# Two steps' horizontal distances and caps in one instruction each, and loads in batches of eight steps, in the main loop of a deformable convolution

## What is computed

```python
py = off_y + hs[None, None, :, None] + ky[None, :, None, None]   # one offset for each tap and pixel
px = off_x + ws[None, None, None, :] + kx[None, :, None, None]
...
return v00 * w00 + v01 * w01 + v10 * w10 + v11 * w11             # bilinear, zero outside the image
...
sampled = sampled * mask[:, None]
out = jnp.einsum('bckhw,ock->bohw', sampled, w.reshape(O, C, KK))
```

## Time and profile before

| | |
|---|---|
| median of 3 runs | 2331.67 us (2330.77 to 2337.22) |
| profiled execution | span 2334.2 us; its own time is not listed apart from the span |
| busy | PE 1539.5 (66%), DVE 1558.4 (67%), ACT 1449.8 (62%), POOL 606.7 (26%) |
| main loop | from about 680 to 2105 us of the span |
| TensorE clock granted, mean | 0.846 |

### The profile page before, as it was taken

One profiled execution on the slowest core, in us unless ns is written; L12 is line 12 of the kernel. 1 busy time (PEld: TensorE's weight loads), 2 busy tenths in 40 slices (PEclk: granted clock), 3 DMA queues, 4 the chain that ended last, 5 costly groups with the idle time before them and its releaser, 6 DMA issues. The chain is left out here.

```text
span 2334.2 us, 61913 instructions
## 1 busy us (share of the span) xinstructions
PE 1539.5 (66%) x24206; PEld 1050.0 (45%) x24207; DVE 1558.4 (67%) x1718; ACT 1449.8 (62%) x2219; POOL 606.7 (26%) x1168
## 2 busy tenths in 40 slices
PE   4755980000008888888898898898888898891620
PEld 4632330000006666666665566666665666660310
DVE  5342006656717888888888788888887888883105
ACT  2221224344218898888898898898887898890102
POOL 2000000000033444444443444444444444430000
PEclk9688995555558999999999999999999999996555
DMA  2177874667675666666666666566666656640008
GB/s 116 32 190 184 233 218 159 215 227 275 235 214 126 151 147 157 149 149 155 150 148 152 148 149 157 149 150 157 149 146 150 152 147 157 149 100 22 3 0 338
DMA packets 288861, 362.19 MB, mean 155 GB/s; under 512 B 61853, under 2 KB 260820, under 8 KB 285014
## 3 DMA queue, kind: packets, MB, share of 16 engines
q1 hardware_dynamic: 209552, 226.57, 37.6%
q0 software_dynamic: 36864, 59.94, 11.2%
q10 hardware_dynamic: 42182, 72.05, 9.0%
HBM read 253.94 MB, written 104.39 MB: 154 GB/s over the span
## 5 line engine op out<-in xcount | busy, mean ns | idle before, releaser
L758 POOL DMA_DIRECT2D rows<-scratch_parts x1152 | 583.1, 514 | 821.1 <-PE ps_even_y L790 798.8
L799 PE MATMUL ps_odd_y<-rows,sel 32*128 32x504 f32 (+2 forms) x928 | 459.8, 496 | 502.5 <-DMA rows<-scratch_parts 345.2
L939 DVE TENSOR_TENSOR G<-odd_y,ps_odd_v 128x1008 f32<-128x1008 f32 (+2 forms) x464 | 542.0, 1168 | 182.5 <-PE ps_odd_v L816 182.4
L816 PE MATMUL ps_odd_v<-tent_x,stage 32*128 32x171 f32 (+2 forms) x5568 | 591.1, 318 | 0.0
L947 DVE TENSOR_TENSOR G<-even_v,ps_even_y 128x1008 f32<-128x1008 f32 (+2 forms) x464 | 539.3, 1162 | 23.6 <-ACT even_v L895 21.7
L816 PE MATMUL ps_even_v<-tent_x,stage 32*128 32x171 f32 (+3 forms) x5568 | 541.9, 324 | 8.5 <-DMA stage<-scratch_xt 8.3
L889 ACT COPY odd_y<-ps_odd_y 128x504 f32<-128x504 f32 (+2 forms) x928 | 526.4, 567 | 21.4 <-PE ps_odd_y L799 17.1
L895 ACT COPY even_v<-ps_even_v 128x1008 f32<-128x1008 f32 (+2 forms) x464 | 450.2, 970 | 134.6 <-PE ps_odd_v L816 126.5
L834 PE MATMUL ps_r<-G,conv_w 128*32 128x224 f32 (+1 forms) x8832 | 483.3, 346 | 13.2 <-ACT res L900 13.1
L799 PEld LDWEIGHTS ps_odd_y<-rows,sel 32*128 32x128 f32 x928 | 173.0, 186 | 689.8 <-issue 350.5
L816 PEld LDWEIGHTS ps_odd_v<-tent_x,stage 32*128 32x128 f32 x5568 | 477.8, 190 | 0.0
(11 more groups left out here) (134 smaller groups left out, 913.5 us busy)
## 6 DMA issues: line engine op xcount, KB each, us to landing
place<-scratch_px SPq DMA_DIRECT2D x960, 105.0 KB, 3.4
scratch_parts<-parts ACTq DMA_DIRECT2D x18, 3136.0 KB, 16.7
rows<-scratch_parts POOLq DMA_DIRECT2D x960, 52.5 KB, 3.4
x<-scratch_xh SPq DMA_DIRECT2D x48, 406.0 KB, 5.9
place<-scratch_px SPq DMA_DIRECT2D x192, 84.0 KB, 2.7
scratch_om<-om ACTq DMA_DIRECT2D x64, 196.0 KB, 7.1
rows<-scratch_parts POOLq DMA_DIRECT2D x192, 42.0 KB, 2.6
scratch_conv<-res SPq DMA_DIRECT2D x448, 14.0 KB, 1.8
```

The lines of the kernel that those rows point to most:

```text
L758: pool.dma_start(bass.AP(tensor=rows[b][:].tensor, offset=32 * g * pitch + here, ap=[[2 * pitch, Y_KINDS], [GROUP * W, 3], [1, count * W]] ...
L799: nc.tensor.matmul(ps_odd_y[:, lo:hi], sel[32 * g:32 * g + 32, :], taps(rows, 32 * g, 32, p, lo, hi), start=True, stop=True).then_inc(odd_ ...
L816: m = nc.tensor.matmul(sub(ps_v[g // 2], 0, 128, i * 512 + lo + first, dims), stage[32 * g:32 * g + 32, j * IMAGE + v * C:j * IMAGE + (v + ...
L939: nc.vector.tensor_tensor(two(G, ROW, v, slot(v)), two(odd_y[p % 3], ROW, v), two(ps_v[1], 512, v), ALU.mult).then_inc(odd_weighted, 1)
```

## The change

`distance` and `cap` now work on a *twin*, two neighbouring steps (2k, 2k + 1) in one instruction of 9 x 112 = 1008 columns, 15 twins a pair with a last one of a single step; `dist_x` and `tent_x` become two buffers of twice the size. Distance and cap stand in steps 1, 3, 5 and so on to 25, for the twin that begins three steps on, and in steps 27 and 28 for the first two twins of the next pair. `sample` reads its half of a twin's tent. `GROUP` becomes 8: four batches a pair of 8, 8, 8 and 5 steps. The tile `zeros` shrinks from 184 to 16 rows, and a transfer that is issued only if some offset reaches far outside the image is cut into pieces.

```diff
...
 RIGHT = 32 - LEFT
 COLUMNS = tuple((first - LEFT, max(0, first - LEFT), min(W, first + RIGHT)) for first in range(0, W, SPAN))
-GROUP = 5
+GROUP = 8
 G_SLOTS = 20
...
         vecs = sb("vecs", 4)
         wm = sb("wm", 128)
-        zeros = sb("zeros", XT_ROWS * C)
+        zeros = sb("zeros", NEAR * C)
 
...
             rows = [sb(f"rows{b}", KK * GROUP * W, f32r) for b in range(2)]
             place = [sb(f"place{b}", KK * GROUP * W) for b in range(2)]
-            dist_x = [sb(f"dist_x{b}", ROW) for b in range(3)]
-            tent_x = [sb(f"tent_x{b}", ROW) for b in range(3)]
+            dist_x = [sb(f"dist_x{b}", 2 * ROW) for b in range(2)]
+            tent_x = [sb(f"tent_x{b}", 2 * ROW) for b in range(2)]
             odd_y = [sb(f"odd_y{b}", 2 * ROW) for b in range(3)]
...
             BATCHES = tuple((first, min(GROUP, STEPS - first)) for first in range(0, STEPS, GROUP))
             ASKED = {first + count - 2: n for n, (first, count) in enumerate(BATCHES)}
+            TWINS = (STEPS + 1) // 2
             block = st.enter_context(nc.Block())
...
                 return first * 3 * W, end * 3 * W
 
-            def both(p):
-
-                return columns(2 * p)[0], columns(2 * p + 1)[1]
+            def twin(it, p):
+
+                return (STEPS + 1) // 2 * it + p // 2
+
+            def twin_steps(p):
+
+                return min(2, STEPS - p)
+
+            def sampled_by(n):
+
+                return STEPS * (n // TWINS) + min(2 * (n % TWINS + 1), STEPS)
+
+            def twin_part(tile, part, parts, p, lo, hi, first, count):
+
+                return sub(tile, part, parts, lo * 2 + p % 2 * W + first, [[2 * W, (hi - lo) // W], [1, count]])
 
...
                     return it, p
                 return None if last else (it + 1, p - STEPS)
+
+            def next_twin(it, p, last):
+
+                if p % 2 == 1 and p + 3 < STEPS:
+                    return it, p + 3
+                if p in (STEPS - 2, STEPS - 1) and not last:
+                    return it + 1, 2 * (p - STEPS + 2)
+                return None
 
...
                             n = ASKED[p] + 2
                             if n < len(BATCHES) or not last:
-                                sp.wait_ge(distant, STEPS * it + p + 2)
+                                sp.wait_ge(distant, twin(it, p + 1) + 1)
                                 load_place(it + n // len(BATCHES), n % len(BATCHES))
...
                         if p == max(0, (first - WIN + 1) // 2):
                             pe.wait_ge(stage_loaded[c], 16 * 4 * len(COLUMNS) * (it + 1))
-                    pe.wait_ge(tent_ready, n + 1)
+                    pe.wait_ge(tent_ready, twin(it, p) + 1)
                     wait(pe, even_kept, n)
...
                             i, v = g % 2, 2 * p + g // 2
                             lo, hi = columns(v)
-                            dims = [[W, (hi - lo) // W], [1, count]]
-                            m = nc.tensor.matmul(sub(ps_v[g // 2], 0, 128, i * 512 + lo + first, dims),
+                            m = nc.tensor.matmul(sub(ps_v[g // 2], 0, 128, i * 512 + lo + first, [[W, (hi - lo) // W], [1, count]]),
                                                  stage[32 * g:32 * g + 32, j * IMAGE + v * C:j * IMAGE + (v + WIN) * C],
-                                                 sub(tent_x[p % 3], 32 * g, 32, lo + first, dims), start=True, stop=True)
+                                                 twin_part(tent_x[twin(it, p) % 2], 32 * g, 32, p, lo, hi, first, count),
+                                                 start=True, stop=True)
                     m.then_inc(sampled, 1)
...
 
                 def distance(it, p):
-                    n = STEPS * it + p
+                    n = twin(it, p)
                     if p % GROUP == 0:
                         k = p // GROUP
                         act.wait_ge(place_loaded[k % 2], 16 * 12 * (len(BATCHES) // 2 * it + k // 2 + 1))
                     wait(act, tent_ready, n - 1)
-                    lo, hi = both(p)
-                    nc.scalar.activation(sub(dist_x[p % 3], 0, 128, lo, [[W, (hi - lo) // W], [1, W]]),
-                                         taps(place, 0, 128, p, lo, hi), ACT.Abs, bias=at[:, 0:1]).then_inc(distant, 1)
+                    dims = [[2 * W, KK], [1, twin_steps(p) * W]]
+                    nc.scalar.activation(sub(dist_x[n % 2], 0, 128, 0, dims),
+                                         sub(place[p // GROUP % 2], 0, 128, p % GROUP * W, [[GROUP * W, KK], dims[1]]),
+                                         ACT.Abs, bias=at[:, 0:1]).then_inc(distant, 1)
 
...
                 distance(0, 0)
                 keep_odd(0, 0, 0)
-                distance(0, 1)
+                distance(0, 2)
                 keep_odd(0, 0, 1)
...
                         if to := ahead(it, p + 1, last):
                             keep_odd(*to, 0)
-                        if to := ahead(it, p + 2, last):
+                        if (to := next_twin(it, p, last)):
                             distance(*to)
...
 
                 def cap(it, p):
-                    n = STEPS * it + p
+                    n = twin(it, p)
                     dve.wait_ge(distant, n + 1)
-                    wait(dve, sampled, n - 1)
-                    lo, hi = both(p)
-                    nc.vector.tensor_scalar(tent_x[p % 3][:, lo:hi], dist_x[p % 3][:, lo:hi], 1.0, 1.0,
-                                            ALU.min, ALU.subtract).then_inc(tent_ready, 1)
+                    if n >= 2:
+                        dve.wait_ge(sampled, sampled_by(n - 2))
+                    if twin_steps(p) == 2:
+                        here = [tile[n % 2][:, :] for tile in (tent_x, dist_x)]
+                    else:
+                        here = [sub(tile[n % 2], 0, 128, 0, [[2 * W, KK], [1, W]]) for tile in (tent_x, dist_x)]
+                    nc.vector.tensor_scalar(here[0], here[1], 1.0, 1.0, ALU.min, ALU.subtract).then_inc(tent_ready, 1)
 
                 cap(0, 0)
-                cap(0, 1)
+                cap(0, 2)
 
                 def body(it, last):
                     for p in range(STEPS):
                         room(it, p)
                         weight_odd(it, p)
                         weight_even(it, p)
-                        if to := ahead(it, p + 2, last):
+                        if (to := next_twin(it, p, last)):
                             cap(*to)
...
                 with sp.If(far > 0):
                     for a, z in ((0, TOP - NEAR), (TOP + H + NEAR, XT_ROWS)):
-                        sp.dma_start(dram("xt", a * C, [[XT_ROW, W], [W * XT_ROW, B], [1, (z - a) * C]]),
-                                     sub(zeros, 0, W, 0, [[0, B], [1, (z - a) * C]])).then_inc(S["x_pads"], 16)
-                    sp.wait_ge(S["x_pads"], 32)
+                        for first in range(a, z, NEAR):
+                            sp.dma_start(dram("xt", first * C, [[XT_ROW, W], [W * XT_ROW, B], [1, NEAR * C]]),
+                                         sub(zeros, 0, W, 0, [[0, B], [1, NEAR * C]])).then_inc(S["x_pads"], 16)
+                    sp.wait_ge(S["x_pads"], 16 * 2 * (TOP - NEAR) // NEAR)
                 sp.nop()
...
```

## The result

The changed kernel takes 2410.8 us (median of 4 runs, 2408.3 to 2412.4) against 2334.4 us of the kernel before on the same chip (4 runs, 2330.8 to 2341.9): ratio 1.032, 95% interval 1.030 to 1.034. It is slower, as forecast, but by 76 us where 9 were forecast, far above the range.

A forecast was written before the change was run, and what follows sets the result against it. Bound: a ring of even copy, first odd copy, second spread and sampling, 2.94 us a step. Terms: -31 (SP's queue) + 26 (late odd copies) + 6.5 (step 3) + 7.5 (start) = +9, forecast 2340 us, range 2316 to 2358.

The forecast's parts named there:

- the queue of SP: Fewer place batches on SP let stores go out sooner, so ACT's result stops waiting for them: 31 us saved.
- I give this nothing: POOL issues four batches of rows loads instead of six, 384 issues fewer; counted as no gain.
- The late odd copy: Longer distance delays ACT's second odd copy, so three-tap steps 8, 12, 16, 20, 24 lose 0.325 each: 26 us.
- 0.05, 0.42 and 1.27: PE's us from second odd copy to first spread, on to the reduction, and on to the second spread.
- Rival 2: The three-tap reduction absorbs the late copy on PE, so the 26 us loss falls away: 2314; chance 0.13.
- Step 3: ACT has a distance and a result in this step: 0.4 us longer, 6.5 us in all.
- Prices: Cost of one 1008-column instruction: distance on ACT 1.145 us (range 1.10 to 1.16), cap on DVE 0.68.
- the cap stayed covered: The longer cap on DVE just fits beside the sampling; if not, up to 15 us lost.
- The start: Before the loop, larger clears (2.5 us) and more bytes to load (5 us) delay the first sampling: 7.5 us.
- 4: Rival: SP's queue stays late as twelve place loads take 8 to 9 us, keeping step 3's waits: 2357; chance 0.2.
- 1: Rival: the slow step 4 at the lower clock goes with the store waits, 13 us less: 2327; chance 0.18.
- 3: Rival: ACT bounds the loop and cheaper instructions pay, 70 us saved: 2262; chance 0.04.

The follow-up runs named there:

- even_batches: The changed kernel with batches of 8, 6, 8 and 7 steps in place of 8, 8, 8 and 5: 2330.1 us, ratio 0.997.
- before_two_results: The kernel before with two result tiles in turn and nothing else: 2295.6 us, ratio 0.982.
- light_loads: The changed kernel with place and rows loads after the first two batches bringing only five of eight steps' bytes: 2337.3 us, ratio 0.999.
- even_moved_two: The changed kernel with batches of 8, 6, 8, 7, two result tiles, and distances in steps 1 and 2 of every four: 2306.3 us, ratio 0.987.
- all_three: The changed kernel with distances moved to steps 1 and 2 of four, two result tiles and a later second place batch: 2374.8 us, ratio 1.015.

## Why the prediction was wrong

**The step that failed is the queue of SP**, "I take them as gone: 44 - 13 = 31 us saved". The order on SP was read rightly, and place batches were issued in the time assumed (5.5 to 7.3 us, and once 9.4, in the turn shown). The waits at step 12 went as forecast, 10 of the 27 us. Those at step 3 did not: they took 16 us before and 23 after. What failed is what stood on the issue times: that a store lands 1.8 us after its issue, the median. The median is still 1.8, but the longest landing has nearly doubled (all stores, in the change and before):

```profile
DMA to landing us min/median/max: 1.4/1.8/10.2
...
DMA to landing us min/median/max: 1.4/1.8/5.5
```

And the store that the result of step 3 waits for, that of step 28, is always among the late ones: over pairs 1 to 15 it lands 6.3 to 9.7 us after the end of its issue (median 8.0), where it took 1.1 to 3.0 before (median 1.1) and takes 1.1 to 2.8 in even_batches (median 1.7).

The prediction had the means to see it: it noted 266 GB/s as the most that the stretch at the start moved, and counted the bytes of a batch. But it never added up who loads when, and said instead that "in the loop these batches now run mostly apart from the rows loads". In the trace place 22 and 27, rows 24 and 0 and two bands of stage fall within 30 us, since the batch of five steps ends early. Disturbance in pairs 1 to 14 is 80 us, where the step left 13.

**POOL, "I give this nothing"**, was the same omission. PE waits for rows only 1.6 us after the change, but these loads are a third of the bytes of place and rows in the crowd.

**PE's stalls for its instructions** were in no rival, and nothing in the trace of before showed one. They are 25 us, and the low clock behind them adds to that.

**The late odd copy**: right, and mis-sized. Predicted 0.325 in steps 8, 12, 16, 20 and 24, measured 0.22 to 0.27: some 20 us for 26. The term that was off is the start of the second odd copy: it follows the start of the distance by 1.04, 0.11 before that one ends, and I had taken over the 0.03 of the 504 form. That 0.03 was no overlap but a wait: in the earlier trace rows the spread that fills the bank ends at 1429.04 + 0.49 = 1429.53, and the copy starts 0.04 later. Behind the longer distance the spread has ended 0.38 earlier, and the copy overlaps ACT's instruction before it by 0.11, as the first odd copy does in the earlier trace rows (1427.51 + 1.00 - 1428.40). 0.05, 0.42 and 1.27 were exact. Rival 2 fell by this. Step 3 costs 0.23, not 0.4. Together 1.3 to 1.5 us a pair for the 2.0 predicted.

**Prices.** The distance and the cap, by form (count, busy us, mean ns, idle before):

```profile
L901 ACT ACTIVATE dist_x<-place,at 128x1008 f32<-128x1008 f32 x224 | 257.3, 1149 | 25.5 <-DMA place<-scratch_px 25.5
...
L981 DVE TENSOR_SCALAR tent_x<-dist_x 128x1008 f32<-128x1008 f32 x224 | 153.4, 685 | 89.4 <-ACT dist_x L901 89.4
```

1.149 against 1.145 taken, 0.685 against 0.68, and the cap stayed covered. The estimate of 1.12 by the Trainium skill (ScalarE: Activation LUTs, What ACT_TABLE_LOAD costs) was 0.03 low, as it was for the 504 form. (A sum of +9 on the median of 2331.7 is 2340.7, not 2340.5; nothing hangs on it.)

**The start**: 11.8 us for 7.5. The clears (2 x 1512 columns are 2.6 us by the earlier trace rows, not the 2.5 put down) came out at nothing, as POOL began 2.2 us sooner; the loads were the larger part. SP and PE after,

```profile
678.82 16.25 SPq L719 DMA_DIRECT2D place<-scratch_px  x24
695.12 21.05 SPq L727 DMA_DIRECT2D stage<-scratch_xt  x48
...
711.93 0.47 PE L836 MATMUL ps_even_v<-tent_x,stage 32*128 32x57 f32 x2 [11.28 <-DMA stage<-scratch_xt]
```

and before:

```profile
678.53 11.29 SPq L698 DMA_DIRECT2D place<-scratch_px  x24
689.86 22.37 SPq L706 DMA_DIRECT2D stage<-scratch_xt  x48
...
700.12 0.47 PE L816 MATMUL ps_even_v<-tent_x,stage 32*128 32x57 f32 x2 [8.30 <-DMA stage<-scratch_xt]
```

Issuing 24 place loads takes 5.0 us more, the 5 that I took; from the first issue of stage to the first sampling it is 16.8 in place of 10.3. That stage lands later because more bytes are queued before it is likely, but no run tests it.

**The rivals.** 4 came nearest: the store waits stayed. Its condition, place batches that take 8 to 9 us to issue, was not what kept them. 1 cannot be judged by the change, where the store waits stayed and 9 of the 14 pairs have a step 4 or 5 of 3.9 us or more. Without store waits 6 pairs have a step of 3.7 us or more there in even_batches, 7 in before_two_results and 11 in light_loads, against 12 before, so it held in part at most. 3 fell: ACT's busy time fell by 54.5 us, and even with the crowd removed nothing of it shows. even_moved_two's loop is 3.8 us shorter in 14 pairs than before_two_results', and its start 9.6 us later.

That the crowd delays stores and brings PE's stalls is shown by the runs in both directions (lighter, and evenly spread). How the DMA engines order an instruction block among the queued loads is not shown; that what PE waits for is an instruction block, late because of them, is argued from the 17 packets and from even_batches. How the 80 us divide among store waits (25.6), stalls (25) and the lower clock is known for the first two alone.

## What to carry to other kernels

Before enlarging a batch of prefetches, write down for every queue which bytes are asked for in which step, over the turn of the loop too, and add them up: a remainder batch puts two full ones next to each other. A median landing time says nothing of the small store that stands behind the burst, and that store may be what an engine waits for. Where a result waits for its predecessor's store, a second result tile costs little: it took 42 us off the kernel before, where the change added 76, and nothing off even_batches, where no such wait was left.

## What the runs showed of the hardware

- While the DMA engines were full, PE stood where no semaphore held it: 0.2 to 2.6 us at a time, 24 times from 810 to 2160 us of the change, each time with a DMA share of 1.03 to 1.11 in the 5 us that end 3 us before PE goes on. One 16 KB packet of the queue "instruction" starts 2.7 to 3.2 us before PE goes on, 24 times of 24. The profile calls the wait "issue".
- A full DMA share alone did not do it: 0.90 to 1.09 over 25 us stayed without a stall in even_batches; 1.03 to 1.12 over 25 us, with two batches of rows in it in place of one, did not. Between these two kernels the landing of the rows loads showed it, 7.3 against 3.4 us for the same 84 KB. It is no sure sign: in all_three the median is 3.5, and PE still stands 9 us.
- In the two turns shown, after a standstill of 2 us or more, PE was granted 0.50 to 0.52 for its next 4 to 7 us of work, and a 24-matmul reduction took 2.47 us in place of 1.34.
